# Macaron network on one core: in the attentions of sixteen narrow heads ScalarE copies the contexts, VectorE divides them at the stage's end

## The reference, cut to what matters

```
scores = jnp.einsum('bhqd,bhkd->bhqk', q, k) / sqrt(8)      # 16 heads, 2048 x 2048
attn = jax.nn.softmax(scores, axis=-1)
ctx = jnp.einsum('bhqk,bhkd->bhqd', attn, v)                # 8 features a head
```

## Time and profile before

| | us |
|---|---|
| median of 3 runs | 3831.17 |
| lowest, highest | 3827.79, 3831.36 |
| profiled execution | 3827.12 |
| its span in the trace | 3825.3 |
| TensorE busy in it | 3500.2 (91%) |
| VectorE | 3040.1 (79%) |
| ScalarE | 2334.5 (61%) |
| GpSimd | 156.0 (4%) |

### The profile page before, as it was taken

One profiled execution on the slowest core, in us unless ns is written; L12 is line 12 of the kernel. 1 busy time (PEld: TensorE's weight loads), 2 busy tenths in 40 slices (PEclk: granted clock), 3 DMA queues, 4 the chain that ended last, 5 costly groups with the idle time before them and its releaser, 6 DMA issues.

```text
span 3825.3 us, 72551 instructions
## 1 busy us (share of the span) xinstructions
PE 3500.2 (91%) x29391; PEld 1429.2 (37%) x29391; DVE 3040.1 (79%) x6567; ACT 2334.5 (61%) x2743; POOL 156.0 (4%) x417
## 2 busy tenths in 40 slices
PE   6989899799999997899999989599997999999988
PEld 4756856522222225122222245222224222222264
DVE  6255855599999964899999747699974999999557
ACT  2232432338888884388888842257784488888832
POOL 0000000200000001000000000200001000000000
PEclk8889999869999998699999989699997799999989
DMA  0010200220000001300000000400002100000000
GB/s 29 5 42 1 76 9 1 58 71 21 2 2 2 2 2 38 94 2 2 2 2 2 2 23 1 121 3 2 2 3 80 44 2 2 2 2 2 4 21 12
DMA packets 33700, 75.94 MB, mean 20 GB/s; under 512 B 10418, under 2 KB 27638, under 8 KB 27990
## 3 DMA queue, kind: packets, MB, share of 16 engines
q1 hardware_dynamic: 33366, 71.30, 6.5%
HBM read 56.54 MB, written 14.73 MB: 19 GB/s over the span
## 4 chain that ended last, share of the span: by engine, by line
DVE 50%; PE 41%; ACT 3%; issue 2%; SPq 2%; POOL 1%; DMA 1%; ACTq 0%; DVEq 0%
DVE pm L2130 43%; PE ps L2064 6%; PE ps L2022 5%; PE ps L1001 4%; PE ps L1004 3%; PE ps L2346 3%; PE ps L1081 3%; PE ps L2367 2%; PE ps L2045 2%; PE ps L1304 2%; SPq L1441 1%; ACT arena L2088 1%; PE ps L2061 1%; PE ps L800 1%; PE ps L1681 1%
## 5 line engine op out<-in xcount | busy, mean ns | idle before, releaser
L2130 DVE TENSOR_REDUCE pm<-ps 128x1 f32<-128x512 f32 x3456 | 2109.5, 684 | 94.2 <-PE ps L2022 89.0
L2088 ACT ACTIVATE arena<-ps 128x1024 f32<-128x1024 f32 (+1 forms) x1856 | 1856.1, 1002 | 437.8 <-PE ps L2045 308.9
L2022 PE MATMUL ps<-arena 64*128 64x512 bf16 (+1 forms) x3712 | 1301.6, 398 | 58.3 <-DMA arena<-parts_dram 43.7
L2064 PE MATMUL ps<-arena,VA 128*16 128x256 f32 (+1 forms) x13824 | 1079.5, 384 | 29.0 <-ACT EV L2109 24.1
L2045 PE MATMUL ps<-arena 64*128 64x512 bf16 (+1 forms) x3520 | 1016.0, 379 | 9.0 <-DMA arena<-m_dram 8.3
L2022 PEld LDWEIGHTS ps<-arena 64*128 64x128 bf16 x3712 | 329.2, 93 | 1112.7 <-DVE pm L2130 860.2
L2064 PEld LDWEIGHTS ps<-arena,VA 128*16 128x16 f32 x13824 | 228.1, 94 | 504.7 <-ACT arena L2088 401.0
L2045 PEld LDWEIGHTS ps<-arena 64*128 64x128 bf16 x3520 | 186.6, 94 | 64.6 <-issue 49.0
L1020 ACT ACTIVATE EV<-ps 128x512 f32<-128x512 f32 x128 | 76.3, 598 | 203.4 <-PE ps L1001 203.4
L1032 DVE TENSOR_TENSOR arena<-EV,ps 128x512 f32<-128x512 f32 x128 | 87.8, 686 | 120.6 <-PE ps L1004 115.5
L1001 PE MATMUL ps<-XNT,arena 128*128 128x512 f32 x304 | 160.9, 612 | 2.3 <-DVE arena L1360 1.5
(11 more groups left out here) (282 smaller groups left out, 2822.8 us busy)
## 6 DMA issues: line engine op xcount, KB each, us to landing
arena<-parts_dram SPq DMA_DIRECT2D x192, 128.0 KB, 2.9
parts_dram<-parts SPq DMA_DIRECT2D x32, 384.0 KB, 2.9
arena<-in_pad SPq DMA_DIRECT2D x16, 512.0 KB, 7.9
arena<-k_dram SPq DMA_DIRECT2D x20, 268.0 KB, 4.2
arena<-in_w SPq DMA_DIRECT2D x4, 1024.0 KB, 5.9
parts<-k_dram SPq DMA_DIRECT2D x8, 268.0 KB, 3.9
arena<-in_w12T SPq DMA_DIRECT2D x1, 2048.0 KB, 9.5
arena<-m_dram SPq DMA_DIRECT2D x122, 6.0 KB
```

Source lines behind the costliest of these rows:

```text
L2022: ins = e.matmul(bank[:, 0:w], QR[half(par), q, 2 * g + pp, qt * P:(qt + 1) * P], KT[half(par), kc, 2 * g + pp, 0:w], start=True, stop=True)
L2064: ins = e.matmul(c.bank(4)[32 * hh:32 * hh + VW, a:b], c.VA[:, j, GH * g + hh, :], self.PB[:, (first + hh) % self.PBS, a:b], start=j == 0 ...
L2088: e.activation(self.PB[:, s:s + 2, offs[0]:CH], c.bank(t % 4, 2).rearrange("p (a t) -> p a t", a=2)[:, :, offs[0]:CH], ACT.Exp, scale=self ...
L2130: e.tensor_reduce(top, bank, AX, ALU.max).then_inc(self.emptied_v.sem, 1)
```

## The change

Three parts.

1. Step `out` goes from VectorE to ScalarE: when the transposes are there, ScalarE copies the sums (128 x 16) into a part of `XN` that is free in this stage, and the undivided contexts (128 x 128) into `CTX`. ScalarE's second copy empties the slot.
2. VectorE divides behind its whole list of steps: for each unit it waits for both copies, inverts the sums in place and multiplies the contexts in place, all in SBUF.
3. In the full attentions, whenever `tick` has run an `out` and maxima are left, one more maximum is laid at once, between the transposes and the values of that tick, and counted in the pacing. The causal attention gets none.

```
     def tick(self, everything=False):
+        ran_out = False
         for item in list(self.later):
             item[0] -= 1
             if item[0] <= 0 or everything:
                 self.later.remove(item)
                 self.run(item[1])
+                ran_out = ran_out or item[1][0] == "out"
+        return ran_out
...
-                    self.tick()
+                    if self.tick() and pending and not self.causal:
+                        self.run(pending.pop(0))
+                        total += 1
...
-        rows = set(self.rows_slot.values())
+        rows = set(self.rows_slot.values()) | set(self.out_slot.values())
...
+        self.sums = chip.XN[:, 3 * TPC:3 * TPC + 2, :].rearrange("p a (b h) -> p (a b) h", h=HEADS)
...
+    def sums_of(self, u):
+        g, q, qa, qb = self.plan.units[u]
+        return self.sums[:, TPC * q + qa:TPC * q + qb, GH * g:GH * g + GH]
+
+    def contexts_of(self, u):
+        g, q, qa, qb = self.plan.units[u]
+        here = self.c.CTX[:, TPC * q + qa:TPC * q + qb, 32 * g:32 * g + 32]
+        return here.rearrange("p q (h d) -> p q h d", d=HD)
...
+            elif step[0] == "out":
+                _, u, slot = step
+                _, _, qa, qb = plan.units[u]
+                here = self.slot_bank(slot)[:, qa * P:qb * P].rearrange("p (q h w) -> p q h w", h=GH, w=32)
+                e.wait_ge(*self.filled[slot])
+                e.activation(self.sums_of(u), here[:, :, :, HD], ACT.Copy).then_inc(self.sums_copied.sem, 1)
+                e.activation(self.contexts_of(u), here[:, :, :, 0:HD], ACT.Copy).then_inc(self.emptied_s.sem, 1)
...
-            elif what == "out":
-                _, u, slot = step
-                g, q, qa, qb = plan.units[u]
-                bank = self.slot_bank(slot)
-                e.wait_ge(*self.filled[slot])
-                if u:
-                    e.wait_ge(*self.emptied(plan.out_slot[u - 1]))
-                here = bank[:, qa * P:qb * P].rearrange("p (q h w) -> p q h w", h=GH, w=32)
-                inverse = c.rd[:, qa * GH:qb * GH].rearrange("p (q h) -> p q h", h=GH)
-                e.reciprocal(inverse, here[:, :, :, HD]).then_inc(self.inverse.sem, 1)
-                e.wait_ge(*self.inverse[u])
-                e.tensor_tensor(
-                    c.CTX[:, TPC * q + qa:TPC * q + qb, 32 * g:32 * g + 32].rearrange("p q (h d) -> p q h d", d=HD),
-                    here[:, :, :, 0:HD], bcl(inverse, HD), ALU.mult).then_inc(self.emptied_v.sem, 1)
+        for u in range(len(plan.units)):
+            sums, contexts = self.sums_of(u), self.contexts_of(u)
+            e.wait_ge(*self.sums_copied[u])
+            e.wait_ge(*self.emptied(plan.out_slot[u]))
+            e.reciprocal(sums, sums).then_inc(self.inverse.sem, 1)
+            e.wait_ge(*self.inverse[u])
+            e.tensor_tensor(contexts, contexts, bcl(sums, HD), ALU.mult).then_inc(self.divided.sem, 1)
```

More of the change, by code:

```diff
@@ L1932, in __init__ @@
         self.filled = sig.claim("slot_filled", p.slots)
-        self.emptied_v = sig.claim("slot_emptied_vector", p.slots - n)
-        self.emptied_s = sig.claim("slot_emptied_scalar", n)
+        self.emptied_v = sig.claim("slot_emptied_vector", p.slots - 2 * n)
+        self.emptied_s = sig.claim("slot_emptied_scalar", 2 * n)
+        self.sums_copied = sig.claim("sums_copied", n)
+        self.divided = sig.claim("contexts_divided", n)
+        self.sums = chip.XN[:, 3 * TPC:3 * TPC + 2, :].rearrange("p a (b h) -> p (a b) h", h=HEADS)
         self.top = sig.claim("maxima_joined", n)
@@ L1943, in __init__ @@
         self.inverse = sig.claim("sums_inverted", n)
-        self.ends = [self.emptied_v[-1], self.emptied_s[-1], self.inverse[-1], self.split[-1], self.copied[-1],
+        self.ends = [self.emptied_v[-1], self.emptied_s[-1], self.inverse[-1], self.divided[-1], self.split[-1], self.copied[-1],
                      self.exped[-1], self.filled[-1], self.valued[-1], self.m_in[0][-1], self.m_in[1][-1]]
```

## The result

| | us |
|---|---|
| before, median of 7 runs | 3830.12 (3827.79 to 3831.36) |
| changed, median of 7 runs | 3843.05 (3840.37 to 3847.90) |
| ratio | 1.0039, 95% interval 1.0029 to 1.0048 |
| profiled execution, before and changed | 3827.12 and 3842.35 |
| forecast | 3845, range 3822 to 3862 |

The page of the changed kernel: the engines, the chain by engine and by line, the costliest group. L2154 is the row maximum (before L2130), L2081 the value products, L2039 the maxima products, L2125 and L2126 ScalarE's two copies.

What follows compares the result with a forecast made beforehand. VectorE's row maxima were taken to bound each attention's first part, TensorE with ScalarE the second. Terms of +4.45 us per full attention made +13.4, +14.1 in all: 3841 profiled, 3845 for the runs, range 3822 to 3862.

Steps and rivals of the forecast that it cites:

- The hole is TensorE's, and the division is hidden in it: Between transposes and next maximum, full attentions: VectorE's 0.51 us division lies in TensorE's hole; removing it alone gives about nothing.
- The extra maximum costs 0.31 on TensorE: Between transposes and value products: the extra product delays what follows by 0.31 us per unit, +4.0 per full attention.
- Thirteen ticks come earlier at 1.09: End of the maxima list: one-maximum ticks begin 13 ticks earlier, at 1.09 instead of 1.20 us, -1.35 per full attention.
- The edges of the TensorE-bound part: Late units, per full attention: context copy +0.3, unit 13's division +0.4, unit 14's +0.3, ScalarE's copies in halved units +0.3 us.
- ScalarE has cover: Steady part: both ScalarE copies, together 0.45 us, fit in 0.81 us of idle between two exps, so are free.
- The end: End of each attention: both copies, then reciprocal and multiply, and a hand-over add 0.5 us before the next stage's first transpose.
- The causal attention: No extra maximum, nothing won: its end costs +0.5 us and its short last units +0.2, bounds -2 to +2.
- Odd ticks cost nothing: Ticks after an odd number of extras, with maxima on swapped halves, take no longer than even ones: no charge.
- Seventeen divisions in a row: Expected sign: VectorE's reciprocals gone from between the maxima, 17 in a row behind the last maximum.
- Rival 2: No change: VectorE's own work sets the extra's cost, +0.09 us per unit, 3834 us; chance 0.22.
- rival 1: Faster: VectorE's own work decides, the 14 divisions in each of three attentions come back, -21.4 us, 3812; chance 0.15.
- rival 4: Odd ticks cost one TensorE pass, 0.23 us, lasting 1.32 instead of 1.196: +80 us in all, 3925; chance 0.04.

Runs made afterwards that it cites:

- e1: The changed kernel without the extra maximum (copies on ScalarE, division at the end): 3828.42 us, ratio 1.0005 to the kernel before.
- e5b: The changed kernel without the extra maximum, with one transpose of four, read four times: 39.13 us per unit, ratio 0.9970 to the kernel before.
- e6b: The kernel before, division still on VectorE, with one transpose of four, read four times: 39.37 us per unit, ratio 0.9973.
- e2: The kernel before with only the extra maximum added, division still on VectorE: 3850.20 us, ratio 1.0054 to the kernel before.
- e7: The changed kernel with two further 512-wide ScalarE copies ahead of the narrow ones in full attentions: 3870.38 us, ratio 1.0110 to the kernel before.
- e8: e3 with the last unit of each attention divided by VectorE out of PSUM: 3823.40 us, ratio 0.9987 to the kernel before.
- e3: The changed kernel with each extra maximum paid back by one fewer 14 ticks later: 3828.97 us, ratio 1.0002 to the kernel before.
- e4: e3 with extra maxima at two more places per unit, each paid back later: 3849.88 us, ratio 1.0056 to the kernel before.

## Why the prediction was right, step by step

- *The hole is TensorE's, and the division is hidden in it.* Shown by e1 (39.39 with neither division nor extra) and by e5b beside e6b. One reading in the argument was off: from the product at 1407.76 to its maximum at 1408.17 it is 0.41, not "the same 0.43". The conclusion holds all the same, as e1's 1.11 shows.
- *The extra maximum costs 0.31 on TensorE.* Forecast unit 39.72, measured 39.74, so 0.335 per unit where 0.31 was charged; the value products came 0.32 behind the extra product. e2 shows the other side: with the division still there VectorE's 0.51 + 0.60 decide, 39.97.
- *Thirteen ticks come earlier at 1.09.* The first maxima 1.09 apart stand at 1369.47 and 1370.56 instead of 1380.28 and 1381.37; 445 exps of the attention have started by then instead of 458, which is 13 ticks. The distance that holds this change of pace is 38.92 instead of 39.41.
- *The edges of the TensorE-bound part.* I added 1.3 us per attention for a context copy, two divisions and ScalarE's copies among the halved units, against 1.35 won by the ticks: -0.05 in all. The thirteenth division lies in the distance that also holds the change of pace, so like is compared with like when all 13 are charged at the measured 0.335: +4.35. The edges are then 38.92 - 39.74 = -0.82, +0.07 and +0.05, in all -0.70 (in the first attention -0.13 stands in place of +0.05). Two errors partly cancel here, and that is luck: the 13 divisions cost 0.3 more than forecast, the edges 0.65 less. For the ticks, the context copy and unit 13's division -0.65 was forecast and -0.75 measured. The mis-sized terms are the other two, unit 14's division and the copies among the halved units: 0.3 charged for each, at most 0.05 seen for both. The tick of that division does last 2.00 between two exps instead of 1.68, but its unit as a whole is hardly longer.
- *ScalarE has cover.* The copies took 0.18 and 0.28 us, as estimated (0.18 and 0.27), and were over 0.48 before they were needed. e7 puts a price on the case where they aren't.
- *The end.* 0.5 forecast, 0.6 to 0.7 measured. e8 takes it away.
- *The causal attention.* 0.2 charged between its copies, -0.3 seen. It varies more than that between kernels whose order in it is the same (391.5 in e1, 394.8 in e3), in single units by steps of 1.3 to 1.5 us (37.20 or 35.73, 7.78 or 6.41); why was not followed up. So the -0.3 can't be read as an effect of the change.
- *Odd ticks cost nothing.* Units with an odd and an even number of extras behind them are both 39.74, within 0.03. The records of the changed kernel show how, which the prediction had not seen. In a tick of an odd unit the score product that carries the signal for the exp, the second in the order, starts right behind the maximum (1030.077 and 1030.083), and the first in the order only at 1030.302; the second maximum follows at 1030.363. So it is in all 32 ticks of that unit, while in an even one the signalling score starts last (1067.536, then 1067.759). The exp still starts behind the end of both (1030.678, exp at 1030.723).
- *Seventeen divisions in a row.* Fifteen came in a row and two later, each as its unit ended. And the gap between the exps was to be no longer than 0.81; it is 1.12. Neither costs anything: VectorE has nothing else to do there, and ScalarE's gap grew by the extra product's 0.31.
- *The sum.* 4.45 per full attention was forecast, 3.6 + 0.6 = 4.2 measured. In all that is +14.1 forecast, and 12.9 between the medians, 15.2 between the profiled executions. Rival 2's floor of 0.09 per unit, rival 1's gain and rival 4's 1.32 us ticks did not come.

## What to carry to other kernels

Before work is taken off the engine that sets the pace, look at what it does next: if the next input is ready only when the work ends, the work is hidden in the feeder's hole, and the hole has to be shortened too. Work put into a hole must be taken out elsewhere, at a place where the buffers are full; laid in as an addition it lengthened the cycle here by about the feeder's cost for it. And with a ring of three buffers the reserve was what three of them hold, not the feeder's idle time over the cycle. What there was to win here was small: the best of these versions is 0.13% faster than the kernel before.

## What the runs showed that I had not expected

The reserve of the full ring is small: a tick that gives VectorE 0.60 us of work in 1.09 costs 0.13 (e3), so full banks cover 0.36 of the missing 0.49. And an extra product at a full ring costs TensorE more than one at an empty ring (0.36 us of waiting at 1090.12 in e4, none at the hole), because everything behind it in TensorE's order waits as well. Nor had I expected that two score products change places in the odd ticks (1030.083 and 1030.302, above).
